# Second layer's attention: exponentials over two heads in four banks of PSUM, maxima over single banks of a ring of two

## What is computed

```python
        scores = jnp.einsum('bhqd,bhkd->bhqk', q, k) * scale
        sparsity = scores.max(axis=-1) - scores.mean(axis=-1)
        _, top_idx = jax.lax.top_k(sparsity, U)
        q_sel = jnp.take_along_axis(q, top_idx[..., None], axis=2)
        scores_sel = jnp.einsum('bhud,bhkd->bhuk', q_sel, k) * scale
        attn = jax.nn.softmax(scores_sel, axis=-1)
        out_sel = jnp.einsum('bhuk,bhkd->bhud', attn, v)
```

## Time and profile before

| | |
|---|---|
| median of 3 runs | 4080.18 us (4068.45, 4080.18, 4084.04) |
| span of the profiled execution | 4082.1 us, mean granted TensorE clock 0.914 |
| PE, PEld, DVE, ACT, POOL busy, whole span | 87%, 53%, 60%, 50%, 31% |
| second layer's attention | 1388 to 1884 us, some 495 us |
| in it, from 1403 to 1880 us (477 us): PE, DVE, ACT, POOL busy | 427.2, 387.4, 336.2, 64.8 us |

### The profile page before, as it was taken

How to read it: one execution, slowest core, us unless ns; L and a number is a source line. 1 busy time by engine, 2 the same in 40 slices (tenths; PEclk the granted TensorE clock), 3 DMA queues, 4 the chain that set the end, 5 groups by cost and what they waited for, 6 DMA issues and landing times. The chain is left out here.

```text
span 4082.1 us, 86911 instructions
## 1 busy us (share of the span) xinstructions
PE 3563.8 (87%) x28212; PEld 2170.8 (53%) x28212; DVE 2450.6 (60%) x5697; ACT 2022.2 (50%) x3970; POOL 1270.3 (31%) x1812
## 2 busy tenths in 40 slices
PE   5799999969996698995999986788986699999997
PEld 2344444436774222222677762368974366666665
DVE  5677777741113688885677776517646566666654
ACT  5466666643335477773233334333344565656562
POOL 0111111100001011110677762605565344444440
PEclk9799999979997799996999997887788799999999
DMA  4322222200001311110666631130005233333330
GB/s 125 83 56 55 57 53 59 48 1 16 11 6 42 79 45 43 41 36 12 174 159 157 160 94 60 36 101 3 3 18 71 86 118 114 118 114 114 118 105 21
DMA packets 198052, 287.18 MB, mean 70 GB/s; under 512 B 40922, under 2 KB 155297, under 8 KB 197461
## 3 DMA queue, kind: packets, MB, share of 16 engines
q1 hardware_dynamic: 193688, 275.28, 24.2%
q0 software_dynamic: 4096, 8.40, 1.4%
HBM read 232.38 MB, written 35.84 MB: 66 GB/s over the span
## 5 line engine op out<-in xcount | busy, mean ns | idle before, releaser
L709 ACT ACTIVATE att_E<-att_pX,att_gs 128x512 f32<-128x512 f32 (+3 forms) x1024 | 723.5, 740 | 421.2 <-PE att_pX L643 176.5
L742 DVE TENSOR_REDUCE att_mx<-att_pS 128x1 f32<-128x512 f32 (+4 forms) x960 | 732.4, 787 | 202.7 <-PE att_pS L617 170.5
L1833 POOL TENSOR_TENSOR att_E<-att_E,att_rz 128x128 f32<-128x128 f32 (+3 forms) x512 | 358.3, 721 | 430.9 <-DVE att_rz L2041 430.9
L637 PE MATMUL att_pX<-arr_qs,arr_ks 75*128 75x512 bf16 (+4 forms) x1536 | 427.3, 334 | 27.6 <-ACT att_E L709 12.6
L612 PE MATMUL att_pS<-arr_ks,arr_qs 72*128 72x512 bf16 (+4 forms) x1536 | 410.3, 339 | 42.9 <-DVE att_pO L732 12.6
L1573 POOL TENSOR_TENSOR pairs_h<-pairs_m,pairs_r 128x512 f32<-128x512 f32 x272 | 346.4, 1274 | 192.0 <-DVE pairs_m L1636 182.9
L574 POOL CAST att_mp<-att_m 16x128 bf16<-16x128 f32 x288 | 81.2, 282 | 932.9 <-DVE att_m L753 907.7
L1597 PEld LDWEIGHTS pairs_po<-pairs_a,pairs_h 128*128 128x128 f32 x2176 | 286.4, 192 | 130.2 <-issue 129.4
L654 PE MATMUL att_pO<-att_E,att_vs 128*9 128x512 f32 (+3 forms) x3072 | 328.6, 500 | 1.3 <-ACT att_E L709 1.3
L1618 ACT ACTIVATE pairs_r<-pairs_ph 128x512 f32<-128x512 f32 x272 | 162.6, 598 | 327.6 <-PE pairs_ph L1589 327.6
L1972 ACT ACTIVATE att_E<-att_S,att_nm 128x128 f32<-128x128 f32 (+3 forms) x512 | 282.1, 556 | 38.6 <-DVE att_nm L2035 38.5
(11 more groups left out here) (411 smaller groups left out, 6551.5 us busy)
## 6 DMA issues: line engine op xcount, KB each, us to landing
pairs_c<-weights SPq DMA_DIRECT2D x272, 256.0 KB, 3.9
att_bias<-in_bias_dram SPq DMA_DIRECT2D x64, 896.0 KB, 4.5
parts<-proj_part SPq DMA_DIRECT2D x144, 128.0 KB, 2.3
att_xb<-xnT SPq DMA_DIRECT2D x64, 256.0 KB, 2.7
arr_qs<-parts SPq DMA_DIRECT2D x192, 64.0 KB
arr_ks<-parts SPq DMA_DIRECT2D x192, 64.0 KB
att_w<-in_w3a_dram SPq DMA_DIRECT2D x64, 192.0 KB, 2.4
arr_qs<-parts SPq DMA_DIRECT2D x96, 96.0 KB
```

Of the source, the lines that this page charges most:

```text
L637: ins = nc.tensor.matmul(dst[:, n], ks[:, g % NB, x, kt * P:(kt + 1) * P], qs[:, g % NB, x, q0(kt):], start=(apart or n == 0), stop=not ca ...
L709: nc.scalar.activation(E[:, kt % 2, WIDE * xp:WIDE * (xp + 1), :w], places(c)[0], ACT.Exp, scale=gs[:, g % 2, gain_of:gain_of + 1]).then_i ...
L742: V.reduce_max(dst, src, AX.X).then_inc(s_mx, 1)
L1833: nc.gpsimd.tensor_tensor(E[:, k, :width(j)], E[:, k, :width(j)], rz[:, u, k:k + 1].broadcast_to([P, width(j)]), ALU.mult).then_inc(s_n, 1)
```

## The change

In the second layer only:

- `WIDE` goes from 1 to 2: an exponential covers 128 x 1024, two heads in two banks; pX now takes four banks (two places of two). A group has 8 exponentials in place of 16.
- A cell of pass 1 is one bank, 128 x 512, in place of two: 16 maxima of 512 elements in a group in place of 8 maxima of 2 x 512. pS takes two banks (two places of one) in place of four.
- `PLAN` puts two cells into each of 8 steps, where before every second of 16 steps had one cell of two banks.
- Routing pieces go one to each of the 8 steps; it is the same 24 pieces in the same three groups of four, behind the same maxima.

```diff
     else:
-        CELLS = [((x, x), j) for x in range(UN) for j in range(0, QT, 2)]
-        PLAN = tuple((s // 2,) if s % 2 == 0 else () for s in range(16))
-        WIDE = 1
+        CELLS = [((x,), j) for x in range(UN) for j in range(QT)]
+        PLAN = tuple((2 * s, 2 * s + 1) for s in range(8))
+        WIDE = 2
...
-        pS = p.ps("pS", [P, 2, T] if causal else [P, 2, 2 * T])
+        pS = p.ps("pS", [P, 2, T])
...
-            if WIDE * w > T or WIDE == 1:
+            if WIDE * w > T:
...
-                        q = j if causal else j + n
+                        q = j
...
-                        dst = mx[:, h % NB, xs[0] * QT + j:xs[0] * QT + j + 2]
+                        dst = mx[:, h % NB, xs[0] * QT + j:xs[0] * QT + j + 1]
...
-                            if aside is not None and s % 2:
-                                aside(dve, i, g * NP2 // 2 + s // 2)
+                            if aside is not None:
+                                aside(dve, i, g * NP2 + s)
```

## The result

The changed kernel takes 4100.81 us (median of 4 runs, 4096.67 to 4108.53), the kernel before 4076.71 us in the same comparison (4 runs, 4068.45 to 4084.04): ratio 1.0059, 95% interval 1.0039 to 1.0079, or +24 us with 16 to 32 as the interval. Slower by a little more than a measurement needs to show it. The forecast was +29 us against its median, 4109.

The account below looks back on a forecast made before the run. Two bounds lay almost level: VectorE in groups with routing, the PE-ACT exchange in those without. Steady +32, start +3 and end -6 us gave +29 on 4080.18, or 4109 us; range 4068 to 4134.

Parts of the forecast that it names:

- The exchange of PE and VectorE through the ring: Second layer's attention, steady groups: PE and VectorE hold each other up over two banks; four groups 61.75 us for 57.43; 56%.
- The chain of 3.49 us: Least time for a pair of slots (steps): PE's 2.21 us between maxima, then two maxima, 1.28 us.
- the other signs: Trace signs: PE's waits for maxima about 100 us, for ACT nearly gone; VectorE's for pass 1 50 or more; ACT's up.
- ring costs nothing: Rival, 21%: in the steady groups VectorE's queue and other work cover PE's 2.21 us; four groups 56.4, total 4069 us.
- A queued maximum of 0.61 us: VectorE's time per queued 512-element maximum; sixteen in place of eight of 1.17 us add 0.4 us per group.
- Each in full: Rival, 8%: the second maximum waits for the first to leave the pipeline, 0.67 us for 0.61; +29 more, 4138 us.
- Steady part: The 30 groups before the last two: +4.3 us per four groups, 7.5 such fours, +32 us.
- Start: 32 maxima of groups 0 and 1, without pass 2: 1.36 us a pair through the ring against 1.17; +3 us.
- The end: Last two groups, without pass 1 and so without ring: about 15.8 us each for 18.75; -6 us for both.
- with PE at half clock: In the last two groups PE's clock is 0.50, matmul times doubled, its own work 15.8 us a group.
- the clock falls: Rival, 8%: a fifth of the stage, 95 us, runs at half clock; +30 more, 4139 us.
- The negation comes later: nothing: Negation one slot's maxima later in a group: its chain is needed six slots, over 10 us, later; no cost.

Follow-up runs that it names:

- pair of narrow kernels: The change with exponentials of one bank again: with a ring of four banks 1.0057, with a ring of two 1.0096, against the kernel before.
- the late turning: Turning of maxima and negation two of sixteen steps later: on the kernel before 0.9941, on one-bank exponentials with a ring of four 0.9952.
- late turning but at the last: Kernel before, turning of maxima and negation two of sixteen steps later, but the last turning at its old place: 0.9941 against the kernel before, -24 us.

## Why the prediction was right, and where not

- **The exchange of PE and VectorE through the ring** was the forecast case, and it came at its size: 62.08 us for 61.75. The chain of 3.49 us is 3.51 in the trace, slot 4's 3.98 is 3.99, the group without routing 14.62 for 14.65, those with routing 15.83 on average for 15.7. PE's wait for the maxima is 306 us, three times what I named; the other signs are there (PE's waits for ACT mostly gone, VectorE's up, ACT's up from 134 to 185 us). The rival "ring costs nothing" fell with the pair of narrow kernels, which differ in the ring alone: 3.8 us in four groups are the ring's.
- **A queued maximum of 0.61 us** was right: a pair takes 1.28, and the eight more a group cost 1.1 us in four groups where the ring is long enough (0.95 with the late turning, 56.98 less 56.03), for 3 x 0.4 = 1.2 forecast in the three with routing. Each in full would have added up to 16 x 0.06 = 0.96 us a group on top there, and that does not show. The rival's price of +29 us was also too high by the prediction's own chain, which holds only two of the four maxima of a pair of slots: 0.67 for 0.61 adds 0.6 us to a group with routing and 0.24 to one without, some 15 us in all (my estimate from the prediction's own terms). The Trainium skill, VectorE: DVE Perf Modes, section The DRAIN you can't avoid, has the rule that the prediction gives, and adds: "A next op that is not held starts earlier". The queued maxima here agree with the addition: two take 1.28 us and not 2 x 0.67 = 1.34. The 125 ns an instruction of the Trainium skill, Perfetto Trace Analysis, section Optimizing Scalar/DVE Operations, give as an estimate 1.0 us a group, 3 us over the three groups in four with routing, where 1.1 was measured.
- **Steady part**: +32 forecast, +35.8 measured. Short falls of the clock make some 2.3 of it: three groups of 17.4 to 17.5 us where their like take 15.9, against two of 15.0 for 13.8 in the kernel before. **Start**: +3 forecast, +2.5 measured; sixteen maxima took 11.04 us, 1.38 a pair for the 1.36 worked out.
- **The end was mis-sized: -6 forecast, -17.9 measured**, with 9.2 us a group for 15.8. The step that failed is "with PE at half clock": I took the 0.50 of the earlier trace rows over into the changed kernel, where it is 1.00. Of the 17.9 us, the clock makes 9.4 (35.6 us at 0.50 and 26.2 at 1.00 for the same narrow groups, in the kernel with late turning but at the last), the wide exponentials 8.4 (26.2 to 17.8). That the trace of before could hardly have told: the rows ahead of the fall name a wait, but putting that wait back once did not bring the fall back.
- So the sum erred by one term that no rival held: the clock as something that the changed kernel gets back, not loses. By these rows the change would have been some 9 us slower still without it. The rival "the clock falls" had the wrong sign. Why the clock stayed up at the change's end is open.
- That +29 lies within 5 us of the measured +24 is partly luck: the steady part was 3.8 us too small and the gain at the end 11.9 too small, so that the stage itself came out at +20.4, and the medians happen to lie 3.7 further apart.
- "The negation comes later: nothing" was true of its chain. What I did not see is that the place of the turning ahead of it was worth 24 us in the kernel before, some 10 in the steady groups and 11 in the last two: I never priced the wait of PE there, because no engine seemed bound by it.

## What to carry to other kernels

A buffer ring is sized by the hand-overs in one turn of the in-order queues around it, not by the busy time of its two ends: add up what stands on the releasing engine's queue between the release and the next use, as here (2.21 + 1.28 us), before giving banks to another engine. If the ring must be short, first move independent work between its two entries: that gave back 18 of 24 us. And look for the in-order engine's wait on the last piece of a batch (the turning of the maxima): a little later it cost nothing, and was worth 24 us in the kernel before, as much as the whole change cost.

## What the runs showed of the hardware

- Granted clock: in the steady part, with PE busy 87% and 90% of four groups in the change and in the kernel before, it still fell to 0.50 for stretches of 3.4 us; in three other kernels it fell for 13.7 us and more (20.5 at the longest); at the end of two kernels it fell for some 30 us. In the kernel with the late turning but at the last, the same two groups ran at 1.00 with PE busy 19.42 of 27.00 us, so there their light load did not bring it down.
- The ring of four was as slow as the change mostly through the clock (groups of 18.8 us for 14.1), and went from +23 to -19 us when one matmul of 0.27 us and the negation behind it were moved a little later in each group.
- Maxima over one bank, queued: 1.28 us for two, where one alone takes 0.67.
